# Graph attention: one scan over pairs in place of two chains of small Vector operations

## The reference

```
e = leaky_relu(s[src] + d[dst], 0.2);  m = segment_max(e, dst)
w = exp(e - m[dst]);  alpha = w / segment_sum(w, dst)[dst]
out += segment_sum(alpha * h[src], dst) + bias
```

## Time and profile before

| | us |
|---|---|
| runs of the kernel | 3779.25, 3785.15, 3970.28 (median 3785.15) |
| profiled execution | 3782.62 |
| its span, first to last instruction | 3780.9 |
| attention turns, first `at_top` to last | 203.6 to 1657.3 |

### The profile page before, as it was taken

The page is one execution under the profiler, slowest core; times in us unless marked ns, Lnnn a source line. Parts: engine busy times, 40 slices in busy tenths (PEclk is TensorE's granted clock), DMA queues, the critical chain, the costliest instruction groups (busy, mean ns, idle before and its releaser), DMA issues. The chain is left out here.

```text
span 3780.9 us, 76143 instructions
## 1 busy us (share of the span) xinstructions
PE 2841.0 (75%) x16134; PEld 2000.5 (53%) x16135; DVE 2309.4 (61%) x8562; ACT 1471.8 (39%) x3352; POOL 2317.7 (61%) x1835
## 2 busy tenths in 40 slices
PE   7267777777777776566699888877878787788763
PEld 4146555555555554442344466666666565666551
DVE  7299999999999997673422354443443443444433
ACT  2055555555555554431000143433433333333331
POOL 0277777777777776510000068888888888888882
PEclk7566666666656665568799889989988988989886
DMA  4544444444444437857034245555555555555544
GB/s 135 102 113 116 128 115 121 122 115 132 120 112 131 115 101 85 101 144 225 3 110 121 71 49 53 54 53 53 54 54 53 54 54 53 54 54 54 54 45 92
DMA packets 659312, 337.65 MB, mean 89 GB/s; under 512 B 434560, under 2 KB 622771, under 8 KB 658228
## 3 DMA queue, kind: packets, MB, share of 16 engines
q0 software_dynamic: 148736, 86.57, 23.9%
q1 hardware_dynamic: 445046, 110.07, 14.2%
q10 hardware_dynamic: 65248, 138.05, 9.8%
HBM read 156.36 MB, written 202.84 MB: 95 GB/s over the span
## 5 line engine op out<-in xcount | busy, mean ns | idle before, releaser
L2183 POOL DMA_INDIRECT sums<-el_rows,el_idx x816 | 1268.6, 1555 | 616.8 <-DVE el_rows L2397 368.6
L822 POOL DMA_INDIRECT at_hs<-table,at_rec_s x976 | 1041.5, 1067 | 444.1 <-PE near_ps L963 216.1
L860 ACT CAST at_count_s<-near_ps 128x400 f16<-128x400 f32 x976 | 482.9, 495 | 732.5 <-PE near_ps L963 644.6
L963 PE MATMUL near_ps<-at_pair_hot,at_src_low_hot 128*128 128x425 f16 x976 | 482.1, 494 | 338.5 <-ACT at_count_s L860 265.7
L2395 DVE CAST el_idx<-el_place 128x4 uint32<-128x4 f32 x204 | 34.8, 171 | 832.5 <-DMA sums<-el_rows,el_idx 812.0
L935 PEld LDWEIGHTS sums_ps<-at_hw,at_hit 128*128 128x128 f32 x1952 | 467.9, 332 | 19.0 <-issue 14.4
L935 PE MATMUL sums_ps<-at_hw,at_hit 128*128 128x66 f32 x1952 | 442.4, 408 | 8.3 <-DVE acc L1009 8.3
L963 PEld LDWEIGHTS near_ps<-at_pair_hot,at_src_low_hot 128*128 128x128 f16 x976 | 134.3, 138 | 485.3 <-ACT at_count_s L860 339.2
L2331 ACT ACTIVATE el_h<-el_h_ps,el_valid 128x128 f32<-128x128 f32 x816 | 232.5, 368 | 248.1 <-PE el_h_ps L2245 248.1
L1001 DVE TENSOR_SCALAR at_pair_hot<-iota_wide,at_rec_s 128x400 f16<-128x400 f16 x976 | 322.4, 333 | 1.4
L1009 DVE SCALAR_TENSOR_TENSOR acc<-acc,at_fade,sums_ps 128x66 f32 x976 | 266.5, 273 | 57.0 <-PE sums_ps L935 52.7
(11 more groups left out here) (374 smaller groups left out, 4980.1 us busy)
## 6 DMA issues: line engine op xcount, KB each, us to landing
slots<-at_count_s ACTq DMA_DIRECT2D x122, 850.0 KB
el_rec<-attr SPq DMA_DIRECT2D x816, 32.0 KB
chunk<-slots SPq DMA_DIRECT2D x256, 100.0 KB
chunk<-slots ACTq DMA_DIRECT2D x208, 100.0 KB
attr<-in_edge_attr SPq DMA_DIRECT2D x16, 1248.0 KB
at_rec_s<-meta SPq DMA_DIRECT2D x976, 3.5 KB
at_hs<-table,at_rec_s POOLq DMA_INDIRECT x976
el_pair<-meta SPq DMA_DIRECT2D x816, 1.0 KB
```

The source lines that it names most:

```text
L822: pool.indirect_dma_start(hs[:, s, u, :], None, k.table, bass.IndirectOffsetOnAxis(rec[:, s, u, 0:1].bitcast(U32), 0)).then_inc(gathered[s ...
L860: a.copy(count[:, (n.o + d) % 2, i, 0:AW], near[:, (n.o + d) % 2, 0:AW]).then_inc(count_ready, 1)
L963: pe.matmul(near[:, s, 0:SW], low_hot[:, s, i, :], pair_hot[:, s, i, :], start=False, stop=True, skip_group_check=(i > 0)).then_inc(near_r ...
L2183: pool.indirect_dma_start(k.sums_flat[a], bass.IndirectOffsetOnAxis(idx[:, j, a:a + 1], 0), rows[:, j, a, :], None, compute_op=ALU.add).th ...
```

## The change

`self_v` goes. Instead `self_top` holds pairs (own score s, best neighbour) per visit, without d, and `fresh` holds pairs (−2^100 or 0, 0). One scan over 16 numbers goes through them: after the first of a pair the state is the maximum before this visit's edges (self edge included), after the second the new one. Adding d (`lrelu` = `run` + `dst_v`) and the leaky ReLU then work on both at once; `fade_in` is the difference of the two. The reduce writes straight into `self_top`.

```diff
-            fresh = k.fresh[:, :, 1:B + 1]
-            v.memset(k.fresh[:, :, 0:1], 0.0).then_inc(fresh_ready, 1)
-            step(v.tensor_tensor(fresh, group_b[:].rearrange("p (n u) -> p n u", u=B),
-                                 prev_b[:].rearrange("p (n u) -> p n u", u=B), ALU.not_equal))
+            fresh = k.fresh[:, :, 0]
+            v.memset(k.fresh[:, :, 1:2], 0.0).then_inc(fresh_ready, 1)
+            step(v.tensor_tensor(fresh, group_b[:], prev_b[:], ALU.not_equal))
...
-            v.tensor_tensor(k.self_v[:], v_ps[:, 0:2, :].rearrange("p i c -> p (i c)"), k.dst_v[:],
-                            ALU.add).then_inc(by_visit_copied, 1)
+            v.tensor_copy(k.self_top[:, :, 0], v_ps[:, 0:2, :].rearrange("p i c -> p (i c)")).then_inc(by_visit_copied, 1)
...
-                    v.tensor_reduce(top[:, s, 1:B + 1], masked[:], AX, ALU.max).then_inc(top_ready, 1)
+                    v.tensor_reduce(k.self_top[:, vis, 1], masked[:], AX, ALU.max).then_inc(top_ready, 1)
...
-                    v.tensor_tensor(top[:, s, 1:B + 1], top[:, s, 1:B + 1], k.dst_v[:, vis], ALU.add).then_inc(best_step, 1)
+                    v.tensor_tensor_scan(run[:, s].rearrange("p u i -> p (u i)"),
+                                         k.fresh[:, vis, :].rearrange("p u i -> p (u i)"),
+                                         k.self_top[:, vis, :].rearrange("p u i -> p (u i)"), run[:, w, B - 1, 1:2],
+                                         ALU.add, ALU.max).then_inc(best_step, 1)
...
-                    v.tensor_tensor(top[:, s, 1:B + 1], top[:, s, 1:B + 1], k.self_v[:, vis], ALU.max).then_inc(best_step, 1)
+                    dve.wait_ge(best_step, n(2, 1))
+                    v.tensor_tensor(lrelu[:, s], run[:, s], k.dst_v[:, vis].unsqueeze(2).to_broadcast([P, B, 2]),
+                                    ALU.add).then_inc(best_step, 1)
...
-                    v.tensor_tensor_scan(run[:, s], fresh, top[:, s], run[:, w, B:B + 1], ALU.add, ALU.max).then_inc(best_step, 1)
+                    dve.wait_ge(best_step, n(2, 2))
+                    v.scalar_tensor_tensor(lrelu[:, s], lrelu[:, s], SLOPE, lrelu[:, s], ALU.mult,
+                                           ALU.max).then_inc(parts_step, 1)
...
-                    v.scalar_tensor_tensor(best[:, s], run[:, s, 1:B + 1], SLOPE, run[:, s, 1:B + 1], ALU.mult,
-                                           ALU.max).then_inc(parts_step, 1)
+                    v.tensor_copy(pick[:, s, 3], lrelu[:, s, :, 1]).then_inc(parts_step, 1)
...
-                    v.tensor_tensor(old[:, s], run[:, s, 0:B], fresh[:, 1:B + 1], ALU.add).then_inc(fade_step, 1)
+                    v.tensor_tensor(fade_in[:, s], lrelu[:, s, :, 0], lrelu[:, s, :, 1], ALU.subtract).then_inc(fade_asked, 1)
...
-                    v.tensor_tensor(old[:, s], old[:, s], k.self_v[:, vis], ALU.max).then_inc(fade_step, 1)
...
-                    v.scalar_tensor_tensor(lrelu_old[:, s], old[:, s], SLOPE, old[:, s], ALU.mult,
-                                           ALU.max).then_inc(fade_step, 1)
...
-                    v.tensor_tensor(fade_in[:, s], lrelu_old[:, s], best[:, s], ALU.subtract).then_inc(fade_asked, 1)
+                    dve.wait_ge(parts_step, n(4, 4))
+                    v.tensor_tensor(pick[:, s, 5], best_rest[:, s], pick[:, s, 4], ALU.subtract).then_inc(pick_ready, 1)
```

More of the change, by code:

```diff
@@ L718, in attention @@
         hit_t = sb("hit_t", [P, 2, B, P], BF16)
[L719 to L722, removed]
+        run = sb("run", [P, 2, B, 2])
+        lrelu = sb("lrelu", [P, 2, B, 2])
         best_rest = sb("best_rest", [P, 2, B])
@@ L725, in attention @@
         drawn = sb("drawn", [P, 2, B, 2])
-        lrelu_old = sb("lrelu_old", [P, 2, B])
         fade_in = sb("fade_in", [P, 2, B])
@@ L739, in attention @@
         gathered = [sem(f"gathered{s}") for s in range(RING)]
-        best_step, fade_step, zed_step, key_step = sem("best_step"), sem("fade_step"), sem("zed_step"), sem("key_step")
+        best_step, zed_step, key_step = sem("best_step"), sem("zed_step"), sem("key_step")
         parts_step = sem("parts_step")
@@ L951, in carries @@
                 else:
-                    pe.wait_ge(run_start, 5)
+                    pe.wait_ge(run_start, 4)
                 for i in range(2):
@@ L1016, in step @@
                 vis = bass.ds(n(B), B) if here else None
-                fresh = k.fresh[:, bass.ds(n(1), 1), :].rearrange("p a u -> p (a u)") if here else None
                 if here:
@@ L1040, in step @@
                 if here:
-                    dve.wait_ge(best_step, n(3, 1))
-                    v.tensor_tensor(top[:, s, 1:B + 1], top[:, s, 1:B + 1], k.self_v[:, vis], ALU.max).then_inc(best_step, 1)
+                    dve.wait_ge(best_step, n(2, 1))
+                    v.tensor_tensor(lrelu[:, s], run[:, s], k.dst_v[:, vis].unsqueeze(2).to_broadcast([P, B, 2]),
+                                    ALU.add).then_inc(best_step, 1)
                 if back:
@@ L1046, in step @@
                 if here:
-                    dve.wait_ge(best_step, n(3, 2))
-                    v.tensor_tensor_scan(run[:, s], fresh, top[:, s], run[:, w, B:B + 1], ALU.add, ALU.max).then_inc(best_step, 1)
+                    dve.wait_ge(best_step, n(2, 2))
+                    v.scalar_tensor_tensor(lrelu[:, s], lrelu[:, s], SLOPE, lrelu[:, s], ALU.mult,
+                                           ALU.max).then_inc(parts_step, 1)
                 if back:
@@ L1052, in step @@
                 if here:
-                    dve.wait_ge(best_step, n(3, 3))
-                    v.scalar_tensor_tensor(best[:, s], run[:, s, 1:B + 1], SLOPE, run[:, s, 1:B + 1], ALU.mult,
-                                           ALU.max).then_inc(parts_step, 1)
+                    dve.wait_ge(parts_step, n(4, 1))
+                    v.tensor_copy(pick[:, s, 3], lrelu[:, s, :, 1]).then_inc(parts_step, 1)
                 if back:
@@ L1059, in step @@
                 if here:
-                    dve.wait_ge(parts_step, n(4, 1))
-                    v.tensor_copy(pick[:, s, 3], best[:, s]).then_inc(parts_step, 1)
-                    v.tensor_tensor(old[:, s], run[:, s, 0:B], fresh[:, 1:B + 1], ALU.add).then_inc(fade_step, 1)
+                    v.tensor_tensor(fade_in[:, s], lrelu[:, s, :, 0], lrelu[:, s, :, 1], ALU.subtract).then_inc(fade_asked, 1)
                     dve.wait_ge(parts_step, n(4, 2))
-                    v.tensor_tensor(best_rest[:, s], best[:, s], pick[:, s, 3], ALU.subtract).then_inc(parts_step, 1)
-                    dve.wait_ge(parts_step, n(4, 3))
-                    v.tensor_copy(pick[:, s, 4], best_rest[:, s]).then_inc(parts_step, 1)
+                    v.tensor_tensor(best_rest[:, s], lrelu[:, s, :, 1], pick[:, s, 3], ALU.subtract).then_inc(parts_step, 1)
                 if next2:
@@ L1074, in step @@
                 if here:
-                    dve.wait_ge(fade_step, n(3, 1))
-                    v.tensor_tensor(old[:, s], old[:, s], k.self_v[:, vis], ALU.max).then_inc(fade_step, 1)
[L1077 to L1080, removed]
-                    v.scalar_tensor_tensor(lrelu_old[:, s], old[:, s], SLOPE, old[:, s], ALU.mult,
-                                           ALU.max).then_inc(fade_step, 1)
+                    dve.wait_ge(parts_step, n(4, 3))
+                    v.tensor_copy(pick[:, s, 4], best_rest[:, s]).then_inc(parts_step, 1)
                 if next2:
@@ L1087, in step @@
                 if here:
-                    dve.wait_ge(fade_step, n(3, 3))
-                    v.tensor_tensor(fade_in[:, s], lrelu_old[:, s], best[:, s], ALU.subtract).then_inc(fade_asked, 1)
+                    dve.wait_ge(parts_step, n(4, 4))
+                    v.tensor_tensor(pick[:, s, 5], best_rest[:, s], pick[:, s, 4], ALU.subtract).then_inc(pick_ready, 1)
                 if next2:
@@ L1117, in _ @@
             v.memset(k.zero_f[:], 0.0).then_inc(run_start, 1)
-            v.memset(run[:, 1, B:B + 1], -BIG).then_inc(run_start, 1)
-            v.memset(top[:, :, 0:1], -BIG).then_inc(run_start, 1)
+            v.memset(run[:, 1, B - 1, 1:2], -BIG).then_inc(run_start, 1)
             v.memset(count[:, :, B, :], 0.0).then_inc(run_start, 1)
@@ L1122, in _ @@
             v.memset(k.out_deg[:], 0.0).then_inc(run_start, 1)
-            dve.wait_ge(run_start, 6)
+            dve.wait_ge(run_start, 5)
             dve.wait_ge(iota_ready, 1)
@@ L2711, in sb1 @@
                     return c1.enter_context(nc.sbuf_tensor(name, shape, dt))
-                k.self_v = sb1("self_v", [P, NV])
+                k.self_top = sb1("self_top", [P, NV, 2])
                 k.dst_v = sb1("dst_v", [P, NV])
                 k.dst_parts = sb1("dst_parts", [P, 3, NV], BF16)
-                k.fresh = sb1("fresh", [P, NV // B, B + 1])
+                k.fresh = sb1("fresh", [P, NV, 2])
                 k.group_v = sb1("group_v", [P, NV])
```

## The result

| | before | after |
|---|---|---|
| median | 3784.04 us | 3748.55 us (3746.07 to 3755.14, 4 runs) |
| ratio | | 0.9913, 95% interval 0.9894 to 0.9933 |
| profiled execution | 3782.62 us | 3747.33 us |

One run of the kernel before took 3970.28 us, the others 3779.25 to 3785.15, and the ratio leaves it out: by the medians the change gains 35 us, by the ratio 33, three times my 11. On the 2% scale it is no change, as forecast; beyond its interval it is a gain.

The account below looks back on a forecast made before the run. DVE bounds attention at 11.51 us a turn, with PE and ACT's exchange next at 11.38. Of 23.9 us over that pace 13.0 stay as jump stalls, so 3782.62 − 10.9 = 3771.7, predicted 3772 us, range 3757 to 3790.

Parts of the forecast that it names:

- my 11: Forecast gain over the 90 attention turns from 325.8 to 1373.9 us: 10.9 us.
- the 2% scale: Whole kernel: within 2% of before counts as no change, chance 0.96; faster or slower by more, 0.02 each.
- DVE sets the pace, at 11.51 us: In the 90 attention turns DVE bounds the kernel before; a plain turn takes 11.51 us.
- The small chain saves 0.58 us, DVE's turn becomes 10.93: DVE from `at_drawn` to `at_miss`: 2.22 us becomes 1.64, four operations fewer, 0.58 us less per turn.
- The scan's 16 numbers: DVE's scan in the small chain: 0.24 us for 9 numbers becomes 0.25 for 16.
- Moved results and the stage before cost nothing: Later `pick_ready` leaves 1.6 us before PE's picks; 1.6 us more before `dst_v` hides under DVE's 2.80 us wait.
- Part of the old wait turns into DVE waiting for ACT's mask: At DVE's opening reduce, 0.45 us per turn becomes waiting for ACT's turned mask.
- the rhythm of three: Repeating pattern of PE and ACT's attention turns: one long, two shorter, three in 34.1 us.
- The ring's pace of 11.38 us: PE and ACT's exchange (matmul, copy, next matmul) in attention: second bound, 11.38 us per turn.
- PE's stalls at the jump stay whole, 13.0 us: PE's three stalls where the attention loop jumps back: 13.0 us together, not gained.
- Rival 1: PE gets more 2.4 GHz in attention turns, DVE bounds again at 10.93: 52 us gained, about 3731; chance 0.09.
- The range: Whole kernel: 3757 to 3790 us, about 8 in 10.

Follow-up runs that it names:

- fill_before: Three spare matmuls of 400 columns per turn on PE, results unused, added to the kernel before; 3780.17 us, ratio 0.9992.
- pad6: Six small Vector operations per turn with unread results added to the changed kernel; 3770.69 us, ratio 0.9972.
- after_again: The changed kernel run once more, not altered; 3754.13 us, ratio 0.9919.
- fill_after: Three spare matmuls of 400 columns per turn on PE, results unused, added to the changed kernel; 3724.99 us, ratio 0.9854.
- fill_more: The changed kernel with four spare matmuls per turn, the fourth of 200 columns before the sixth count; 3714.37 us, ratio 0.9823.
- shorter: The changed kernel without the second and third bfloat16 part of the maximum on DVE; 3752.07 us, ratio 0.9931.
- fill_shorter: The changed kernel without the maximum's second and third bfloat16 part, plus three spare matmuls per turn; 3714.70 us, ratio 0.9827.

## Why the prediction was wrong

- *DVE sets the pace, at 11.51 us:* right. fill_before shows it: a quicker PE is worth nothing there.
- *The small chain saves 0.58 us, DVE's turn becomes 10.93:* right, 10.93 measured. That it fits to the hundredth is luck: the stretch took 1.59 us for my 1.64, so it lost 0.63 us while the whole turn lost 0.58.
- *The scan's 16 numbers:* 0.23 us for my 0.25; no longer than for 9.
- *Moved results and the stage before cost nothing:* right; PE doesn't wait at the picks for `pick_ready`, and DVE still waits 2.72 us for PE where the longer memset had to be hidden.
- *Part of the old wait turns into DVE waiting for ACT's mask:* right in kind. I said 0.45 us per turn; it is 26.4 us in 90 turns, 0.29, because the ring was quicker. In the stretch of the rhythm of three, from 325 to 530 us, it is 8.9 us at 19 reduces, 0.47.
- ***The ring's pace of 11.38 us*, the failed step.** I took it from two places of three turns each and called it "the same rhythm of three". Both showed the rhythm of three. It is one of two; that of four, at 11.09, was seen with a DVE turn of up to 11.16 us and not with 11.30. In the loop of the kernel before, DVE at 11.51 us did not let it run. Where it holds, a turn is 0.29 us shorter, and that is 17 of the missing 20 us. pad6, where DVE leaves hardly any but the rhythm of three, gives the predicted time within 2 us. A sign of it stood in the trace of the kernel before, in the four turns just ahead of the three that I read:

```profile
234.97 0.83 PE L954 MATMUL near_ps<-at_count_s,carry_by 128*128 x2 [0.71 <-ACT at_count_s L860]
...
279.88 0.89 PE L954 MATMUL near_ps<-at_count_s,carry_by 128*128 x2 [0.71 <-ACT at_count_s L860]
```

These are four turns in 44.91 us, 11.23 each, none of them wholly at 1.2 GHz: the granted clock was 0.66, 0.65, 0.62 and 0.68.
- *PE's stalls at the jump stay whole, 13.0 us:* PE's idle time there did, 13.6 us. But the three turns with a jump are only 10.8 us longer than 3 × 11.38, some 3 us that I had not counted as gained. What makes up for the rest of the stall was not looked into.
- *Rival 1*, a ring with more of the high clock, had 0.09. It is what happened in part: in the rhythm of four the granted clock is 0.65 in the mean, in that of three 0.60, but DVE doesn't bound again. Over 326 to 1320 us it rose only from 0.62 to 0.64, and in after_again it stayed at 0.62, so the mean over a long stretch doesn't show it. The Trainium skill ("TensorE: Matmul & The Clock Gate", "Part 1: The HAM clock gate"), by which activity releases the throttle, spoke for it, and fill_after and fill_more agree, with 0.71 and 0.76. I set the rule aside for an average over three turns.
- The range was too narrow by the same step: it gave the ring's pace 8 to 14 us of gain, as if only the share of long turns in the rhythm of three could vary, and had no case with some of rival 1.

## What to carry to other kernels

When the engine that bounds gets faster, the gain ends at the second bound; measure that bound at several places, all those where nothing else holds it, and ask whether it can itself move, above all when it holds matmuls whose granted clock changes from turn to turn. Two bounds close together hide each other (here 10.93 us a turn against 11.09 and 11.38): a cut that is worth nothing (shorter) pays once the other bound is lowered (fill_shorter). Before giving up on a ring of PE and another engine that wait for each other, fill PE's waits with spare matmuls and look at the granted clock; but first make sure that the ring sets the pace, since in fill_before the same matmuls gained nothing.

## What the runs showed of the hardware that I had not expected

- One ring of PE and ACT ran in two rhythms, three turns in 34.1 us (granted clock 0.50, 0.65, 0.65) or four in 44.3 us (0.66, 0.62, 0.68, 0.65). Two executions of the same program differed by 15 us, 7 of them in the 90 turns where the rhythms changed.
- Spare matmuls with unused results made the kernel 24 us (three per turn) and 34 us (four) faster, at a granted clock of 0.71 and 0.76 instead of 0.64.
- Independent operations on 8 numbers per partition started 0.08 us apart on DVE, half their duration of 0.16 us, and each made DVE's turn 0.06 to 0.07 us longer (0.20 us for three, 0.37 for six, 0.67 for ten). A scan over 16 numbers in pairs took no longer (0.23 us) than one over 9 (0.24).
